# A ring of 16 for the first FFN chunks, a new beginning, one projection a group and another order in the attention slots

## The reference

```python
x = x + 0.5 * ffn(layernorm(x))
x = x + attention(layernorm(x))
x = x + 0.5 * ffn(layernorm(x))

def ffn(x):        # 16 experts of 64 columns, 4 picked a token, and a shared one of 128
    scores = sigmoid(x @ gate_kernel) + gate_bias       # groups of 4 experts: the best 2 groups stay
    combine = 2.5 * picked / (sum(picked) + 1e-20)      # top 4 experts, else 0
    y_e = (silu(x @ w_gate[e]) * (x @ w_up[e])) @ w_down[e]
    return sum(combine[e] * y_e) + (silu(x @ sw_gate) * (x @ sw_up)) @ sw_down

def attention(x):  # 16 heads of 8, one shared k and v of 8 features, |i - j| <= 32 alone counts
    logits = einsum('btnh,bsh->bnts', q, k) / sqrt(8)
    return einsum('btns,bsh->btnh', softmax(masked(logits)), v) @ Wf.T + bf
```

## Time and profile before

| | us |
|---|---|
| median of 3 runs | 331.09 |
| lowest, highest | 330.57, 335.35 |
| the profiled execution | 330.3 |
| its span | 328.5 |

### The profile page before, as it was taken

How to read it: one execution, slowest core, us unless ns; L and a number is a source line. 1 busy time by engine, 2 the same in 40 slices (tenths; PEclk the granted TensorE clock), 3 DMA queues, 4 the chain that set the end, 5 groups by cost and what they waited for, 6 DMA issues and landing times.

```text
span 328.5 us, 4752 instructions
## 1 busy us (share of the span) xinstructions
PE 277.2 (84%) x1404; PEld 181.9 (55%) x1404; DVE 186.0 (57%) x583; ACT 150.3 (46%) x285; POOL 139.7 (43%) x167
## 2 busy tenths in 40 slices
PE   0768759999989996688886898595988999999995
PEld 0646327666656654354563474263865766766662
DVE  1586432848982467559466558642366485494230
ACT  3556134456432225546546746565263544632220
POOL 4710377155743597145134142400233816652740
PEclk9989969999999999979999899999799999999999
DMA  6300907255956833644865732103500801703511
GB/s 180 111 0 5 308 17 266 71 134 142 245 137 215 209 64 106 159 73 147 157 99 151 154 68 56 39 19 77 185 1 4 257 0 52 239 3 105 187 32 32
DMA packets 44355, 37.00 MB, mean 113 GB/s; under 512 B 18888, under 2 KB 32810, under 8 KB 44330
## 3 DMA queue, kind: packets, MB, share of 16 engines
q1 hardware_dynamic: 43306, 36.44, 41.5%
q0 software_dynamic: 1024, 0.26, 0.4%
HBM read 31.76 MB, written 4.84 MB: 111 GB/s over the span
## 4 chain that ended last, share of the span: by engine, by line
PE 56%; DVE 17%; issue 10%; ACT 8%; DMA 4%; POOL 2%; SPq 1%; DVEq 0%; ACTq 0%; POOLq 0%
PE pY L957 14%; PE pY L1043 4%; PE pU L1030 4%; PE pG L875 3%; DVE ring L740 3%; PE pG L876 3%; PE pG L877 3%; PE pU L876 3%; PE pU L877 3%; PE pU L875 3%; PE pG L1015 3%; PE p L1085 3%; DMA X<-x 2%; DVE neg_max L777 2%; SPq L281 1%
## 5 line engine op out<-in xcount | busy, mean ns | idle before, releaser
L459 POOL TENSOR_TENSOR ring<-ring,c_all 128x512 f32<-128x512 f32 x64 | 80.7, 1280 | 74.6 <-DMA c_all<-comb_dram 40.0
L740 DVE TENSOR_TENSOR ring<-ring,pU 128x512 f32<-128x512 f32 x72 | 49.2, 684 | 60.6 <-PE pU L877 41.0
L535 ACT ACTIVATE ring<-pG 128x512 f32<-128x512 f32 x72 | 42.6, 597 | 80.1 <-PE pG L877 76.0
L957 PE MATMUL pY<-ring,wd_sb 128*128 128x512 f32 x144 | 74.7, 612 | 2.8 <-POOL ring L459 2.7
L875 PE MATMUL pG<-xt_hi,wg_hi 128*128 128x512 f32 x72 | 53.3, 740 | 2.0 <-ACT ring L535 1.9
L571 ACT ACTIVATE probs<-pU 128x512 f32<-128x512 f32 x64 | 34.6, 595 | 9.6 <-PE pU L1030 9.4
L777 DVE TENSOR_REDUCE neg_max<-pG 128x8 f32<-128x768 f32 x32 | 30.5, 952 | 10.2 <-PE pG L1015 9.9
L957 PEld LDWEIGHTS pY<-ring,wd_sb 128*128 128x128 f32 x144 | 25.8, 193 | 13.3 <-issue 5.8
L875 PE MATMUL pU<-xt_hi,wu_hi 128*128 128x512 f32 x72 | 29.2, 406 | 2.4 <-DVE ring L740 2.4
L1015 PE MATMUL pG<-k_diag,q_rep 128*128 128x384 f32 x64 | 21.1, 411 | 9.8 <-issue 5.1
L876 PE MATMUL pG<-xt_hi,wg_lo 128*128 128x512 f32 x72 | 29.2, 406 | 0.0
(11 more groups left out here) (137 smaller groups left out, 425.1 us busy)
## 6 DMA issues: line engine op xcount, KB each, us to landing
c_all<-comb_dram SPq DMA_DIRECT2D x64, 256.0 KB, 4.3
q_stage<-q_dram SPq DMA_DIRECT2D x16, 192.0 KB
q_t<-q_dram SPq DMA_DIRECT2D x16, 192.0 KB
k_diag<-k_dram SPq DMA_DIRECT2D x32, 72.0 KB
q_dram<-q_hi SPq DMA_DIRECT2D x8, 256.0 KB, 3.0
q_t<-qrows_dram SPq DMA_DIRECT2D x2, 576.0 KB
X<-x SPq DMA_DIRECT2D x4, 256.0 KB, 3.9
q_dram<-q_lo SPq DMA_DIRECT2D x4, 256.0 KB, 3.0
```

The source lines that it names most:

```text
L459: pool.tensor_tensor(ring[:, n % RING], ring[:, n % RING], c_all[:, n % CH], ALU.mult)\
L535: act.activation(ring[:, n % RING], pG[:, n % 2], ACT.Silu).then_inc(silu_done, 1)
L740: dve.tensor_tensor(ring[:, n % RING], ring[:, n % RING], pU[:, n % 2], ALU.mult).then_inc(gu_done, 1)
L957: pe.matmul(pY[:, u % 2], wd_sb[:, D * e:D * (e + 1)], ring[:, n % RING], start=e == 0, stop=e == CH - 1)\
```

## The change

The ring of the first FFN pass gets 16 places. Chunks 8 to 15 use the area of the raw weights (`raw`, the same memory as the attention's probabilities); `extra(n)` holds back the hid and the down of the first chunks, so that down 0 and 1 stand in slot 15 and then two downs a slot until they have caught up. PE starts with four matmuls on zeros; ACT makes the first high parts of the weights ahead of the first normalizing, half of which moves to DVE; of the rstd chain only the power stays on POOL; all low parts of the weights are made on DVE. The SP queue loads all weights and blocks first, then the attention constants, and only then the combine weights of unit 0. Routes are spread over more slots. A projection is now one 128x128 matmul a group; DVE adds it to `X`, and POOL adds the bias once a block. In an attention slot weighted_values is split around the second half of the scores, copy_o follows the exps on ACT, max_rows stands ahead of normalize_attention on POOL, and layer norms and route steps stand at the end of DVE's slot. Attention slots 17 to 20 and FFN2 slots 0 to 3 alternate from slot 18 on.

```diff
-RING, CRING = 8, 8
+RING, DEEP, CRING = 8, 16, 8
...
-    for t in range(NG + 3):
+    for t in range(NG + 2):
         order.append((ATTN, t))
         order += late[2 * t:2 * t + 2]
-    order += [(FFN2, 0), (ATTN, NG + 3)]
-    order += [(FFN2, s) for s in range(1, SLOTS)]
+    for t in range(3):
+        order += [(FFN2, t), (ATTN, NG + 2 + t)]
+    order += [(FFN2, s) for s in range(3, SLOTS)]
...
+X_STATS = {(FFN1, 3): 1, (FFN1, 12): 2, (FFN1, 16): 3, (ATTN, 9): 4, (ATTN, 14): 5, (FFN2, 7): 6, (FFN2, 16): 7}
+X_SHIFT = {(FFN1, 4): 1, (FFN1, 13): 2, (FFN1, 17): 3, (ATTN, 10): 4, (ATTN, 15): 5, (FFN2, 8): 6, (FFN2, 17): 7}
+X_NORM = {(FFN1, 5): 1, (FFN1, 14): 2, (FFN1, 18): 3, (ATTN, 10): 4, (ATTN, 16): 5, (FFN2, 9): 6, (FFN2, 18): 7}
...
+ROUTE = {(FFN1, 0): (0, 0, 3), (FFN1, 1): (0, 3, 6), (FFN1, 2): (0, 6, 9), (FFN1, 4): (0, 9, 12),
+         (FFN1, 5): (0, 12, 14), (FFN1, 6): (0, 14, 17), (FFN1, 7): (0, 17, 19), (FFN1, 8): (0, 19, 21),
+         (FFN1, 9): (1, 0, 3), (FFN1, 10): (1, 3, 6), (FFN1, 11): (1, 6, 9), (FFN1, 13): (1, 9, 14),
+         (FFN1, 14): (1, 14, 18), (FFN1, 15): (1, 18, 21),
+         (FFN1, 17): (2, 0, 7), (FFN1, 18): (2, 7, 14), (FFN1, 19): (2, 14, 21),
+         (ATTN, 13): (4, 0, 7), (ATTN, 14): (4, 7, 14), (ATTN, 15): (4, 14, 21)}
...
+COMB = {(FFN1, 8): 0, (FFN1, 16): 1, (FFN1, 20): 2, (FFN1, 26): 3, (ATTN, 16): 4, (FFN2, 8): 5, (FFN2, 17): 6,
         (FFN2, 26): 7}
...
-PROJECT = {(ATTN, 7): 0, (ATTN, 11): 1, (ATTN, 15): 2, (ATTN, 19): 3}
+BIAS = {(FFN1, 33): 0, (ATTN, 1): 1, (ATTN, 5): 2, (ATTN, 9): 3}
...
-FIRST_DELAY = (3, 2, 2, 1, 1)
+def extra(n):
+    return max(0, DEEP - 1 - DOWN_LAG + n // 2 - n)
...
+        def ring_at(n):
+            return raw[:, (n - RING) * SEQ:(n - RING + 1) * SEQ] if RING <= n < DEEP else ring[:, n % RING]
...
-                if i == 0:
-                    sp.dma_start(gbias_sb[:], gbias).then_inc(route_in, 16)
-                    sp.dma_start(tri[:], tri_in).then_inc(route_in, 16)
-                    sp.dma_start(X[:, 1], x_t[1]).then_inc(x_in[1], 16)
+            sp.dma_start(gbias_sb[:], gbias).then_inc(route_in, 16)
+            sp.dma_start(tri[:], tri_in).then_inc(route_in, 16)
+            sp.dma_start(X[:, 1], x_t[1]).then_inc(x_in[1], 16)
             for i in range(3):
                 sp.dma_start(third(wd_sb, i), third(wd, i)).then_inc(wd_in[i], 16)
+            for b in (2, 3):
+                sp.dma_start(X[:, b], x_t[b]).then_inc(x_in[b], 16)
...
-            combine_weights(0)
-            for b in (2, 3):
-                sp.dma_start(X[:, b], x_t[b]).then_inc(x_in[b], 16)
-            combine_weights(1)
...
-            combine_weights(2)
             sp.wait_ge(diag_zeroed, 1)
...
+            combine_weights(0)
+            combine_weights(1)
+            combine_weights(2)
             sp.wait_ge(pads_in, 16)
+            combine_weights(3)
             store_q(0)
             store_k(0)
-            combine_weights(3)
...
             def rstd_of(r):
-                pool.wait_ge(mv_done, NT * (r + 1))
-                pool.tensor_tensor(var_eps[:], mv[:, :, 1], eps[:], ALU.add).then_inc(eps_done, 1)
+                pool.wait_ge(eps_done, r + 1)
                 wait(pool, xn_done, NT * r)
-                pool.tensor_tensor(minus_mean[:], mv[:, :, 0], minus[:], ALU.mult).then_inc(minus_done, 1)
-                pool.wait_ge(eps_done, r + 1)
                 pool.tensor_tensor(rstd[:], var_eps[:], half[:], ALU.pow).then_inc(rstd_done, 1)
-                pool.wait_ge(rstd_done, r + 1)
-                pool.wait_ge(minus_done, r + 1)
-                pool.tensor_tensor(shift[:], minus_mean[:], rstd[:], ALU.mult).then_inc(shift_done, 1)
...
+            def add_bias(a):
+                pool.wait_ge(axn_done, a + 1)
+                pool.wait_ge(attn_w_in, 4 * 16)
+                pool.tensor_tensor(X[:, a], X[:, a], bias_sb[:].unsqueeze(1).to_broadcast([P, NT, D]), ALU.add)\
+                    .then_inc(bias_added, 1)
...
+                if kind == ATTN and 1 <= t <= NG:
+                    max_rows(t - 1)
                 if slot in XA_NORM:
                     normalize_attention(XA_NORM[slot])
-                if kind == ATTN and 1 <= t <= NG:
-                    max_rows(t - 1)
+                if slot in BIAS:
+                    add_bias(BIAS[slot])
                 if slot in Q_SPREAD:
                     spread_q(*Q_SPREAD[slot])
...
+                if n == RING:
+                    act.wait_ge(w_lo_dve, 6)
+                elif n >= DEEP:
+                    act.wait_ge(down_done, n - (DEEP if n < DEEP + RING else RING) + 1)
+                act.activation(ring_at(n), pG[:, n % 2], ACT.Silu).then_inc(silu_done, 1)
...
+                if n == 0 and i == 0:
+                    act.wait_ge(down_done, DEEP)
                 act.activation(probs[:, n % 2, i], pU[:, i % 2], ACT.Exp).then_inc(exp_done, 1)
...
-                if kind == ATTN and 0 <= t - 3 < NG:
-                    copy_o(t - 3)
                 if kind == ATTN and 0 <= t - 2 < NG:
                     exps(t - 2, 2)
                     exps(t - 2, 3)
+                if kind == ATTN and 0 <= t - 3 < NG:
+                    copy_o(t - 3)
                 if kind == ATTN and 0 <= t - 4 < NG:
                     output_columns(t - 4)
...
+                dve.tensor_scalar(var_eps[:], mv[:, :, 1], EPS, None, ALU.add).then_inc(eps_done, 1)
+            def shift_of(r):
+                dve.wait_ge(rstd_done, r + 1)
+                dve.scalar_tensor_tensor(shift[:], mv[:, :, 0], -1.0, rstd[:], ALU.mult, ALU.mult)\
...
+            def add_attention(n):
+                a, g = divmod(n, G4)
+                dve.wait_ge(attn_psum, n + 1)
+                dve.wait_ge(bias_added, a + 1)
+                dve.tensor_tensor(X[:, a, g], p1[:, P:2 * P], X[:, a, g], ALU.add).then_inc(attn_added, 1)
...
+            dve.memset(ring[:, 0], 0.0).then_inc(warm, 1)
...
+            shift_of(0)
+            for t in range(NT // 2, NT):
+                dve.tensor_scalar(xn[:, t], X[:, 0, t], mv[:, t, 0:1], rstd[:, t:t + 1], ALU.subtract, ALU.mult)\
+                    .then_inc(xn_done, 1)
+            weights_lo(0)
+            weights_lo(1)
             columns_lo(0)
-            dve.wait_ge(w_hi_done, 2)
-            dve.tensor_tensor(third(wu_lo, 0), third(wu_raw, 0), third(wu_hi, 0).bitcast(F32), ALU.subtract)\
-                .then_inc(w_lo_dve, 1)
+            weights_lo(2)
...
+                if kind == ATTN:
+                    if slot in X_STATS:
+                        layernorm(X_STATS[slot])
+                    if slot in XA_STATS:
+                        attention_layernorm(XA_STATS[slot])
+                    if slot in ROUTE:
+                        r, lo, hi = ROUTE[slot]
+                        for k in range(lo + 1, hi + 1):
+                            route(r, k)
...
-            def project(a):
-                pe.wait_ge(ot_copied, G4 * (a + 1))
-                for g in range(G4):
-                    for i in range(2):
-                        for b in range(2):
-                            rows = slice(64 * b, 64 * (b + 1))
-                            ins = pe.matmul(p0[rows, P * g:P * (g + 1)], o_t[rows, g, 64 * i:64 * (i + 1)],
-                                            wf_sb[rows, i], start=False, stop=g == G4 - 1 and i == 1)
-                ins.then_inc(attn_psum, 1)
+            def project(n):
+                pe.wait_ge(ot_copied, n + 1)
+                pe.matmul(p1[:, P:2 * P], o_t[:, n % NQ], wf_sb[:], start=True, stop=True).then_inc(attn_psum, 1)
+            pe.wait_ge(warm, 1)
+            for _ in range(4):
+                pe.matmul(pY[:, 1], ring[:, 0, 0:P], ring[:, 0], start=True, stop=True)
...
+                if kind == ATTN and 0 <= t - 5 < NG:
+                    project(t - 5)
                 if kind == ATTN and 0 <= t - 4 < NG:
                     output_to_rows(t - 4)
+                if kind == ATTN and 0 <= t - 3 < NG:
+                    weighted_values(t - 3, 0)
                 if kind == ATTN and t < NG:
                     scores(t, 1)
                 if kind == ATTN and 0 <= t - 3 < NG:
-                    weighted_values(t - 3)
+                    weighted_values(t - 3, 1)
                 if kind == ATTN and 0 <= t - 2 < NG:
```

251 lines of the change are left out of this document (105 added, 146 removed).

## The result

| | median us | range of the runs |
|---|---|---|
| before | 332.16 | 330.57 to 335.35 (4) |
| the change | 337.88 | 336.76 to 339.23 (4) |
| the change, profiled execution | 336.76 | span 335.0 |

The ratio is 1.0226 (95% interval 1.0168 to 1.0284): slower by 2.3%, where I had forecast 2% faster. The time lies outside my range (314 to 334). Some executions of every kernel are disturbed and slower; the ratios compare undisturbed ones, and from the profiles of e1, e3, r6, x1 and z6, which are of disturbed ones, I take waits and durations and not the total. My slower case had put 339 on a late `c_all`; the time is near it, the cause is another.

The account below looks back on a forecast made before the run. PE was taken as the bound in full FFN stretches, so gains had to come from its waits. Terms -10.5 +2.5 +2.4 -1.2 +1.5 +3.2 +2.8 +1.5 -2.2 -5.6 = -5.6 gave 324.7, median 325 us, range 314 to 334.

Parts of the forecast that it names:

- What bounds: TensorE (PE) bounds the full FFN stretches; gains must come where PE waits: start, attention slots, passage into the second FFN.
- Six of the seven steps: Stretches between PE marks from start to second FFN, forecast -0.75, -7.25, +2.4, +0.3, +3.2, +2.1 and -5.6 us.
- Point 1: Start of the first FFN: deep ring and new beginning, -10.5 us, with PE waiting 4.2 before the first down.
- rival D: First FFN: DVE starves behind POOL, costing +7 instead of +2.5, total 330 us; chance 0.19.
- Point 2: First FFN: denser DVE work beside POOL's hids makes two stalls that PE sees, +2.5 us, bounds 0 and +7.
- Point 3: SP queue before scores(0): store_q(0) behind the combine weights of unit 3 delays scores(0), +2.4 us with half clock.
- Point 4: Attention slots: block 1 -1.2, block 2 +1.5, slot 9 +3.2, slot 14 +2.8 and clock after it +1.5 us.
- point 5: Attention slots: one projection a group, single matmuls of 0.25 to 0.3 us, 1.1 a block; -2.2 for block 2.
- Point 6: Passage into the second FFN: 13.1 us becomes 7.5, output steps hidden under the gate/ups, -5.6 us.
- C: Start: first-pass weights (c_all) come so late that the deep ring only moves the wait, 339 us; chance 0.09.

Follow-up runs that it names:

- e1: The change, with POOL's memset of k_diag begun only after the four xn tiles of unit 0: 331.25 us, ratio 0.998 to the kernel before.
- e3: The change, with store_q(0) and store_k(0) ahead of the combine weights of unit 3 on the SP queue: 338.73 us, ratio 1.018.
- r6: The change with the edits of e1 and e2, and unit 0's combine weights ahead of attention weights and rows on the SP queue: 335.31 us, 1.009.
- x1: r7 with both layer norms back in the middle of DVE's attention slot, as before the change: 323.01 us, ratio 0.963.
- z6: z4 with copy_o again between the two pairs of exps on ACT: 323.25 us, ratio 0.965, of medians alone.
- z3: The change, with only the low parts of wkv and wq moved from slot 18 to slot 22 on DVE: 330.75 us, ratio 0.995.
- r7: The change with the edits of e1 and e2, and the low parts of wkv and wq in slot 22: 322.15 us, ratio 0.970.
- x3: The kernel before, with blocks 2 and 3 of x loaded right behind wd: 325.77 us, ratio 0.978.
- e2: The change, with max_rows ahead of the power of the X norm on POOL in attention slots: 327.71 us, ratio 0.987.
- r8: The change, with the layer norm of X back at its old place in DVE's attention slots: 327.87 us, ratio 0.987.
- z4: r7 with weighted_values in one piece behind the second half of the scores: 319.89 us, ratio 0.955.
- z1: r7 with each group's projection computed twice into the same place: 325.65 us, ratio 0.983.
- x5: The change, with the slots at the passage into the second FFN as before: 335.24 us, ratio 1.008.

## Why the prediction was wrong

Two steps failed most: the first `xn` on DVE, a gain of 0.75 that became a loss of 3.9, and the attention slots, +5.6 that became +12.3. **What bounds** and the method held: PE's chain in the full FFN stretches, waits at the same five places. Six of the seven steps with a forecast had the right sign.

**Point 1 failed, in the smallest term.** I had taken half of the normalizing to DVE and priced it at ACT's 0.48 a step, for a gain of 0.75. It cost 3.9. My own forecast named the memset nowhere, although it stood on POOL from 6.62 to 11.8 in the profile of the kernel before, across the very microseconds to which the steps were moved. The matmuls on zeros, put at no cost and no gain, are worth about 1.3 us by these rows when `xn` comes in time (e1); no run leaves them out. What I called the path, "they take part of it back", had no look at the other engine. e1 shows the cause. The queue part (rows, `c_all`) was right within 2.5 us. (My row of 60 to 68 us took in the first `q_t` rows, issued at 66.02; from 64 to 66, with `k_t` alone, the share is 0.14 and 41 GB/s, so the reading holds.)

The Trainium skill (SBUF — State Buffer, section "Who interferes with whom") says that a copy, cast or `tensor_scalar` of DVE that runs in a two-port mode takes the pair of ports it shares with GpSimd, and that then the later of the two waits for the whole instruction of the other. The rows agree: 5.74 against 0.60, though no row shows the mode of the step. It also says that a step with two SBUF inputs meets only those GpSimd operations that read. The rows agree there too: in the kernel before, a step with two SBUF inputs ran at its own speed (0.54 behind the memset in the change) in the middle of the same memset (timelines of DVE and of POOL),

```profile
8.80 0.56 DVE L813 TENSOR_TENSOR wg_lo<-probs,wg_hi 128x384 fp32r<-128x384 f32 x1 [3.88 <-ACT wg_hi L590]
```
```profile
6.62 5.21 POOL L481 MEMSET k_diag<- 128x6144 f32 x1
```

while `wkv_lo` took 1.45 beside hids and 0.28 alone. I had used the second half of this rule (rival D) and missed the first.

**Point 2 was right in kind and too small.** I had +2.5. From logits(0) to gate(34) the step came within 0.3 us of my sum by luck, because two errors met: PE began 3.9 us late and so found `c_all` there (no wait of 4.2), and DVE behind POOL cost more. z3 prices one place at 3.4 us at gate(21). Case D, with +7, described this part better than my forecast did. With the memset and the two DVE steps mended (r7) gate(34) is 8.9 ahead of the kernel before, and my points 1 and 2 together had said 8.0: with these two places out the beginning as a whole did what I had said. How much of it the deep ring makes is not shown; x3 gets 7.2 without it.

**Point 3 had the right size and the wrong cause.** +2.3 against +2.4; but the order of the queue, to which I had put it, saves 2 (e3). I put it down to the move of the q projection by two slots, a row of a table that I had not priced; no run tests that.

**Point 4 failed by half.** Its five terms were +7.8 together; with point 5 the slots to keys(15) cost +12.3 against a forecast of +5.6. The mechanism was the forecast one, and e2 and r8 confirm it from two sides. Its size was off because I let the slots "catch up" behind the wait: PE waited 8.92 us and then ran at the lower clock. From 187.80 to about 194 each pair of key matmuls takes 1.06 to 1.19 us instead of 0.7. In the slots 5 and 6 of block 1, where I had a gain of 1.2, the attention's own layer norm at the slot's end makes a wait of 2.52 for `neg_max`: the same mistake of the change at a place that I had looked at only from its good side. And I had put copy_o behind the exps at nothing, since "ACT's copy has a slot of slack"; z4 and z6 show that it has none in a slot that nothing else delays: 0.33 a slot for copy_o (I had named 0.6 as the price of that case), and 0.33 for the split, which I had not priced.

**Point 5** had the price right: from a projection to the next matmul it is 0.32 us, and 0.22 for one more (z1), against my 0.25 to 0.3. A block's projection work is so 0.9 to 1.3 us against 2.3 before, and the wait of 1.09 for `o_t` is gone. But every group's projection now stands in the ring of waits of its slot, which I did not see. How much of the -2.2 arrived can't be told: it lies in a step that lost 3.5 by the longer wait at keys(13) and the clock of 0.77 behind it (219.7 to 230.5).

**Point 6** was forecast -5.6 and is -3.9, of which x5 puts 0.5 on the slots. What failed is the hiding: I had put the outputs' ACT and DVE steps under the gate/ups, and PE waits for `o_norm` twice between them (1.36 at 239.06, 1.44 at 243.31). gate(0) to gate(3) take 11.9 us, not 7.5.

**The cases.** C had the right time by a late `c_all` that did not occur here; r6 shows that it can. The point that none of my cases had is that the beginning, which I treated as nearly free, could itself be the first to slip.

**Open.** Why the granted clock from scores(0) to keys(15) is 0.83 to 0.89 in every version of the change (0.88 and 0.89 in e2, r7, r8, x1 and z1) and 0.95 to 0.97 in every version of the kernel before, also where its waits are as long. 3.6 us more work on PE did not raise it (z1), nor did the old order of the slot (z4). What is left untried is the projection's own form, once a group against once a block. It costs: PE is busy some 5 to 10 us longer for about the same work.

## The version that beats both

r7, the change with three edits, takes 322.15, 0.970 of the kernel before (0.962 to 0.979) and about 5% under the change; z4, with weighted_values whole besides, 319.89 and 0.955 (0.942 to 0.969), which the intervals don't part from r7. x3, two lines of the kernel before moved, already reaches 0.978. Deep ring, new beginning and one projection a group are together worth 1 to 2% over that, and the intervals touch.

## What to carry to other kernels

Before a step is moved to another engine, read what its neighbour does in those microseconds, and price the step by the longest thing there: 0.60 us of DVE work took 5.74 beside a memset. An instruction that waits for a late input is a wall for all behind it on its engine: a power of 1.0 us ahead of two DMA issues made PE wait 8.92. And try the cheapest part of a large change by itself first: two loads that stood too late in a queue held most of what the deep ring was built for.

## What the runs showed of the hardware that I had not expected

Two DVE `tensor_scalar` steps on 128x128 f32 last 5.74 us beside a POOL memset of 128x6144 and 0.60 without it, while `tensor_tensor` with two SBUF inputs is not held by that memset (0.56) but by a POOL multiply that reads (1.36 and 1.45 against 0.28). And the placing of `c_all` loads behind slow row loads costs by the unit: 3.4 us gained at unit 0 came back as a wait of 14.9 at unit 1.
